# Second layer's queries and keys projected ahead of its loop and fetched per batch

## The chip, the cores and the metric

One core of a Trainium2 chip runs the whole program in one launch. The metric is device time in microseconds (us). Engines: PE (TensorE, with its weight loads PEld), DVE (VectorE), ACT (ScalarE), POOL (GpSimd), and SP, which here only issues DMAs. Each engine takes its instructions in order and waits on semaphores for the others.

## The reference, cut to what matters

Two transformer layers over x of 32 batches x 256 rows x 128 features, with a layer norm behind each of the four parts:

```python
# layer 0: x = LN(x + attention(x)); qkv with bias and a low-rank part, 16 heads of depth 8
# then     x = LN(x + experts(x)):
probs = softmax(x @ gate_w.T); top2_w, top2_idx = top_k(probs, 2)
counts = bincount(a_e, length=E); keep = counts <= cap      # cap = 1.25 * rows / E
contrib = y[a_e, p] * (a_w * valid)                         # 0 for an expert over its capacity
# layer 1: x = LN(x + attention(x)), causal, no bias, queries and keys rotated:
q = q * cos + _rotate_half(q) * sin
k = k * cos + _rotate_half(k) * sin
att = softmax(where(causal, q @ k.T * scale, min)); y = (att @ v) @ w_proj
# then     x = LN(x + ffn(x)), a spline feed-forward part
```

## The kernel before, in words

x lies in SBUF as 64 tiles of 128 rows (x_all, x_mid); a batch is two tiles. Five stages follow each other: `prepare`, `attention` for layer 0 (attn0), `moe`, `attention` for layer 1 (attn1), `spline_ffn`.

`attention` is a software pipeline over batches: step b works on batch b (transpose x, project queries and keys, split each into three bf16 parts and send them through DRAM, whence they come back stacked in q_st and k_st, L215), on batch b-2 (scores by rows, L558, and their maximum on DVE, L376), on b-3 (scores by columns, L580, exponential on ACT, L317, sums of values, L597) and on b-4 (normalise, output projection L537, residual L429, layer norm). Steps 0 to 4 fill it, a hardware loop of three steps a round follows, and some written-out steps drain it at the end. Within a step PE, ACT and DVE go through 16 turns n = 0 to 15 (one head or one half of two heads each); the table `AT` says at which turn each other piece comes. PE holds the row scores in three PSUM banks (`ROW_BANKS`): rows(u) waits until DVE's row_max(u-3) is done. cols(n) waits for the exponential n-2.

In attn1 before, for batch b of step b: SP copies x from x_mid into x_in (L195); PE transposes it at n = 0 (L481) into in_ps; ACT copies it to xT (L323); PE projects queries and keys at n = 1 (L502) into in_ps; ACT, at n = 2, writes q_half with the two halves of the partitions exchanged (L339, two copies of 64x512) and qk (L345, two of 128x256); POOL waits for these four (`qk_kept`) and then multiplies q_half by sin (L261), qk by cos (L262), adds (L265), and splits (L271 to L283). PE's value projection (L524, n = 4) waits for the same four copies, since it writes in_ps. At the end of each step, behind that work, POOL makes the variance and rstd of batch b-4 (L289, L291, a power). DVE's order at n = 15 is: row_max(15), residual and statistics (L429, L433), split of the maxima (L387, L389), aggregate (L439), and the two L444, which wait for rstd and write x_mid; row_max(0) of the next step stands behind them. In attn0 the layer norm is made by POOL instead (L297, L301).

`moe`: SP copies x_all in groups of eight tiles (L748), PE transposes them (L785), projects the gates (L797) and transposes back (L807); DVE measures mean and variance (L727 to L735) and copies logits (L868). Then one chain on DVE over all 64 tiles finds the two best experts and their counts (L876 to L903), PE adds the counts, and DVE makes a flag (L907 to L909): is any expert within its capacity? ACT (L845) and DVE (L915) write x_mid, the second layer norm. A second block does the experts' work if the flag is set; here it isn't.

## Time and profile before

| | us |
|---|---|
| median of three runs (lowest, highest) | 1361.35 (1359.0, 1361.97) |
| the profiled execution, its own time | 1361.33 |
| its span, first to last instruction | 1359.6 |
| layer 0's attention ends, moe begins | 540.5, 541.8 |
| layer 1's attention begins | 591.3 |

| engine | busy us | share of the span |
|---|---|---|
| PE | 1081.3 | 80% |
| DVE | 1029.6 | 76% |
| ACT | 835.7 | 61% |
| POOL | 582.8 | 43% |

A share of the whole span mixes stages: read it by stretch. In a timeline row stand the start and the length in us, the engine, the line, the operation, out<-in, partitions x elements, how many instructions were merged (x2), and in brackets how long the engine had been idle and who ended that. The duration of a row is that of the merged run.

### The profile page before, as it was taken

The page shows a single profiled execution, that of the slowest core. Times are in us where ns is not written, and L with a number is a line of the kernel's source. Part 1 is how long each engine was busy: PE and PEld are TensorE (multiplying, and loading weights), DVE is VectorE, ACT ScalarE, POOL GpSimd, SP SyncE. Part 2 cuts the span into 40 slices and gives each one's busy share as a digit, 9 for nine tenths or more (in the row PEclk, how much of TensorE's full clock was granted, in tenths as well). Part 3 has the DMA queues.
Part 4 walks back from the last instruction along what each step waited for, and adds up shares of the span by engine and source line. Part 5 has one row for each costly group of instructions (what it writes and reads, how often), then busy time and mean ns, then how long its engine had stood idle before and what let it go on. Part 6 is the DMA issues. An engine that isn't in the chain of part 4 may idle for free. (4 is left out here: it accounts for less than half of the span.)

```text
span 1359.6 us, 36441 instructions
## 1 busy us (share of the span) xinstructions
PE 1081.3 (80%) x11411; PEld 799.5 (59%) x11411; DVE 1029.6 (76%) x2823; ACT 835.7 (61%) x1904; POOL 582.8 (43%) x696
## 2 busy tenths in 40 slices
PE   2699999999999996516999999999999996501330
PEld 1366666666666663314888888888888873201220
DVE  3578888888888883824787788877888763698885
ACT  1267777777777774552666776767767664401675
POOL 3234434444444432434555555555555506000776
PEclk9799999999999998756999999999999998855555
DMA  2655555565556540305444554444554412100011
GB/s 57 151 122 136 131 139 128 133 140 131 136 135 137 135 100 10 115 29 134 120 119 121 119 123 120 116 121 119 124 119 120 115 35 82 43 0 0 24 47 54
DMA packets 122613, 137.33 MB, mean 101 GB/s; under 512 B 12562, under 2 KB 110258, under 8 KB 113330
## 3 DMA queue, kind: packets, MB, share of 16 engines
q1 hardware_dynamic: 121506, 136.50, 40.6%
q8 instruction: 34, 0.56, 0.2%
q14 instruction: 33, 0.27, 0.1%
q10 hardware_dynamic: 1040, 0.00, 0.0%
HBM read 85.03 MB, written 37.75 MB: 90 GB/s over the span
## 5 line engine op out<-in xcount | busy, mean ns | idle before, releaser
L376 DVE TENSOR_REDUCE attn_negmax<-attn_row_ps 128x2 f32<-128x512 f32 (+1 forms) x1024 | 597.8, 618 | 151.4 <-PE attn_row_ps L558 136.4
L317 ACT ACTIVATE attn_probs<-attn_col_ps 128x512 f32<-128x512 f32 (+1 forms) x1024 | 534.9, 546 | 111.8 <-PE attn_col_ps L580 106.5
L558 PE MATMUL attn_row_ps<-k_st,q_st 72*128 72x256 bf16 (+1 forms) x2048 | 370.3, 263 | 14.9 <-DMA k_st<-attn_scratch 13.9
L580 PE MATMUL attn_col_ps<-q_st,k_st 74*128 74x256 bf16 (+1 forms) x2048 | 369.8, 262 | 2.6 <-ACT attn_probs L317 2.0
L597 PE MATMUL attn_out_ps<-attn_probs,v_sb 128*32 128x256 f32 (+1 forms) x4096 | 230.4, 358 | 0.7 <-ACT attn_probs L317 0.7
L580 PEld LDWEIGHTS attn_col_ps<-q_st,k_st 74*128 74x128 bf16 x2048 | 184.3, 99 | 73.9 <-ACT attn_probs L317 23.2
L558 PEld LDWEIGHTS attn_row_ps<-k_st,q_st 72*128 72x128 bf16 x2048 | 201.9, 99 | 41.3 <-issue 15.3
L597 PEld LDWEIGHTS attn_out_ps<-attn_probs,v_sb 128*32 128x32 f32 x4096 | 123.3, 110 | 71.2 <-issue 21.3
L554 PE MATMUL attn_row_ps<-mask_qk,ident_h 128*128 128x256 bf16 x512 | 141.5, 276 | 19.1 <-DMA k_st<-attn_scratch 18.0
L576 PE MATMUL attn_col_ps<-mask_kq,ident_h 128*128 128x256 bf16 x512 | 141.3, 276 | 1.2 <-ACT attn_probs L317 1.0
L289 POOL TENSOR_SCALAR attn_var<-attn_mv 128x2 f32<-128x2 f32 x64 | 14.3, 223 | 265.8 <-DVE attn_mv L439 265.8
L276 POOL TENSOR_TENSOR attn_rest<-attn_qk,attn_parts 128x512 f32<-128x512 f32 x64 | 73.9, 1154 | 122.8 <-DVE attn_mparts L389 118.0
L261 POOL TENSOR_TENSOR attn_q_half<-attn_q_half,sin 128x512 f32<-128x512 f32 x32 | 40.7, 1273 | 136.4 <-ACT attn_qk L345 136.4
L502 PE MATMUL attn_in_ps<-attn_xT,wqk 128*128 128x256 f32 x256 | 79.6, 437 | 2.4 <-ACT attn_xT L323 2.4
L1552 POOL TENSOR_TENSOR ffn_rstd<-ffn_var,minus_half 128x8 f32<-128x8 f32 x19 | 31.8, 1674 | 106.6 <-DVE ffn_var L1574 105.2
L283 POOL TENSOR_TENSOR attn_parts<-attn_rest,attn_parts 128x512 bf16<-128x512 f32 x64 | 73.9, 1154 | 5.4
L271 POOL TENSOR_SCALAR attn_parts<-attn_qk 128x512 bf16<-128x512 f32 x64 | 39.5, 617 | 63.1 <-ACT attn_qk L342 49.2
L554 PEld LDWEIGHTS attn_row_ps<-mask_qk,ident_h 128*128 128x128 bf16 x512 | 49.6, 97 | 28.7 <-issue 18.7
L1482 PE MATMUL ffn_o_ps<-ident_h,ffn_onehot 128*128 128x128 bf16 x64 | 10.0, 312 | 70.2 <-PEq L1233 70.2
L1493 PE MATMUL ffn_r_ps<-table_hm,ffn_ohT 128*128 128x193 bf16 x64 | 21.0, 361 | 55.8 <-ACT ffn_ohT L1505 55.8
L356 ACT COPY attn_onT_sb<-attn_fin_ps 128x256 f32<-128x256 f32 x64 | 23.7, 370 | 60.2 <-PE attn_fin_ps L531 60.2
L576 PEld LDWEIGHTS attn_col_ps<-mask_kq,ident_h 128*128 128x128 bf16 x512 | 49.6, 97 | 16.1 <-issue 6.5
(230 smaller groups left out, 1689.0 us busy)
## 6 DMA issues: line engine op xcount, KB each, us to landing
q_st<-attn_scratch SPq DMA_DIRECT2D x192, 192.0 KB
k_st<-attn_scratch SPq DMA_DIRECT2D x192, 192.0 KB
attn_scratch<-attn_parts SPq DMA_DIRECT2D x64, 384.0 KB, 2.8
attn_scratch<-attn_parts SPq DMA_DIRECT2D x64, 128.0 KB, 2.9
x_in<-in_L_attn_x_dram SPq DMA_DIRECT2D x32, 128.0 KB, 2.6
x_all<-in_L_attn_x_dram SPq DMA_DIRECT2D x32, 128.0 KB, 7.0
moe_xs<-x_all SPq DMA_DIRECT2D x8, 512.0 KB, 2.9
x_in<-x_mid SPq DMA_DIRECT2D x32, 128.0 KB, 2.4
```

Source lines behind the costliest of these rows:

```text
L261: nc.gpsimd.tensor_tensor(q_half[:, :, :], q_half[:, :, :], sin, ALU.mult).then_inc(sin_done, 1)
L271: nc.gpsimd.tensor_scalar(parts[:, :, 0, :], qk[:, :, :], 1.0, 0.0, ALU.mult, ALU.add)\
L276: nc.gpsimd.tensor_tensor(rest[:, :, :], qk[:, :, :], parts[:, :, 0, :], ALU.subtract)\
L283: nc.gpsimd.tensor_tensor(parts[:, :, 2, :], rest[:, :, :], parts[:, :, 1, :], ALU.subtract)\
L317: nc.scalar.activation(probs_of(st, 3, u)[:, j, 0:W], col_ps[:, n % 2, 0:W], ACT.Exp, scale=scale).then_inc(probs_kept, 1)
L376: nc.vector.tensor_reduce(negmax[:, t, 2 * p:2 * p + 2], row_ps[:, row_bank(st, u), 0:2 * keys].rearrange("p (a k) -> p a k", a=2), AX_X, ...
L502: last = nc.tensor.matmul(in_ps[:, s * N:(s + 1) * N], wqk[:, s, :], xT[:, st.slot(0), :], start=True, stop=True)
L554: nc.tensor.matmul(seen[:, :, keys - P:keys], ident_h[:, :], mask_qk[:, :, :], start=True, stop=False, skip_group_check=True)
L558: last = nc.tensor.matmul(bank[:, a * keys:(a + 1) * keys], q_st[0:KROWS, sl, h, t * P:(t + 1) * P], k_st[0:KROWS, sl, h, 0:keys], start=n ...
L576: nc.tensor.matmul(seen[:, :, 0:P], ident_h[:, :], mask_kq[:, :, :], start=True, stop=False, skip_group_check=True)
L580: last = nc.tensor.matmul(bank[:, t * N:(t + 1) * N - first], k_st[0:rows, sl, h, t * P:(t + 1) * P], q_st[0:rows, sl, h, first:N], start= ...
L597: last = nc.tensor.matmul(out_ps[32 * j:32 * j + 32, g * N + first:(g + 1) * N], v_sb[:, st.slot(lag), t, 32 * h:32 * h + 32], probs_of(st ...
```

## The change

It has four parts. (1) In attn0 POOL, behind each batch's layer norm, works out the reciprocal deviation that the second layer norm will have (from rstd and the variance, `r_mid`) and writes x_mid = x_all * r_mid at once. (2) `moe` has no statistics, no copies through SP and no layer norm of its own: PE transposes x_mid straight into xT_all, which takes x_all's place in SBUF, and the logits are multiplied by 1/r_mid. The groups are written out; ACT copies the logits; the routing chain runs in two halves of 32 tiles. If the flag is set, x_all is restored and the transposes are made again. (3) attn1 has no transposes and no projection of queries and keys in its loop. Ahead of it PE projects batches 0 to 19 from xT_all into col_ps, and batches 20 to 31 in step 2, one a turn, n = 0 to 11. ACT copies 0 to 2 to qk and q_half; the others go into the buffers of probs and from there, four batches to a DMA from ACT's queue, to DRAM. (4) In the loop SP copies xT (128 KB) at a step's start and fetches qk of the next batch (256 KB) behind the six stack loads; ACT writes q_half from qk at n = 14; qk and q_half have three slots, so POOL waits only for copies made one step ahead (`half_kept`). DVE's copy of the values moves from n = 4 to 5.

```diff
@@ AT, attn1
-      "attn1": dict(act_xT=0, act_mT1=1, act_qk=(2, 2), act_oT=(4, 5), act_onT=13, act_mT0=9,
-                    dve_o=9, dve_split0=7, dve_split1=15, dve_v=4, dve_y=15, dve_var=15, dve_ln=15,
-                    pe_xT=0, pe_mT1=2, pe_qk=1, pe_oT=7, pe_v=4, pe_onT=11, pe_mT0=9, pe_y=15,
+      "attn1": dict(act_mT1=1, act_oT=(4, 5), act_half=14, act_onT=13, act_mT0=9,
+                    dve_o=9, dve_split0=7, dve_split1=15, dve_v=5, dve_y=15, dve_var=15, dve_ln=15,
+                    pe_mT1=2, pe_oT=7, pe_v=4, pe_onT=11, pe_mT0=9, pe_y=15,
...
+FRONT_GROUP = 4
+FRONT_EARLY = 20
@@ attention, sync
+            def load_xT(st):
+
+                if st.has(3):
+                    sp.wait_ge(v_ready, st.seq(3, c=1))
+                sp.dma_start(xT[:, st.slot(0), :], xT_all[:, bass.ds(st.seq(0), 1), :].rearrange("p b n -> p (b n)"))\
+                    .then_inc(x_loaded[st.slot(0)], 16)
+
+            def load_qk(st):
+
+                sp.wait_ge(rest_kept, st.seq(2, c=1))
...
+                sl = st.slot(-1)
+                of = qk_dram[bass.ds(st.seq(-1), 1)].rearrange("b p n -> (b p) n")
+                sp.dma_start(qk[:, sl, :, :].rearrange("p s n -> p (s n)"), of).then_inc(qk_loaded[sl], 16)
...
+                if fronted and st.has(-1) and (st.loop or st.off >= AHEAD):
+                    load_qk(st)
@@ attention, gpsimd
-                    pool.wait_ge(qk_kept, st.seq(0, QKOPS, QKOPS))
+                    if not fronted:
+                        pool.wait_ge(qk_kept, st.seq(0, QKOPS, QKOPS))
+                    elif st.loop or st.off >= SLOTS:
+                        pool.wait_ge(half_kept, st.seq(SLOTS, 2, 2))
+                    else:
+                        pool.wait_ge(front_kept, kept_by(st.off))
...
+                        nc.gpsimd.tensor_tensor(square[:, :], rstd[:, :], rstd[:, :], ALU.mult).then_inc(again, 1)
+                        pool.wait_ge(again, st.seq(4, 5, 1))
+                        nc.gpsimd.tensor_tensor(square[:, :], square[:, :], mv[:, :, 1], ALU.mult).then_inc(again, 1)
+                        pool.wait_ge(again, st.seq(4, 5, 2))
+                        apart(pool, mem)
+                        nc.gpsimd.tensor_scalar(square[:, :], square[:, :], EPS, 0.0, ALU.add, ALU.add)\
+                            .then_inc(again, 1)
+                        pool.wait_ge(again, st.seq(4, 5, 3))
+                        r_mid = mem["r_mid"][:, bass.ds(st.seq(4, TB), TB)]
+                        nc.gpsimd.tensor_tensor(r_mid, square[:, :], mem["minus_half"][:, 0:TB], ALU.pow)\
+                            .then_inc(again, 1)
...
+                        nc.gpsimd.tensor_tensor(mem["x_mid"][:, bass.ds(st.seq(4, TB), TB), :],
+                                                x_all[:, bass.ds(st.seq(4, TB), TB), :],
+                                                r_mid.unsqueeze(2).broadcast_to([P, TB, C]), ALU.mult)\
+                            .then_inc(again, 1)
@@ attention, scalar
+            def front(b):
+
+                act.wait_ge(front_ready, b + 1)
+                of = col_ps[:, b % 2, :]
+                if b < SLOTS:
+
+                    nc.scalar.copy(qk[:, b, :, :].rearrange("p s n -> p (s n)"), of).then_inc(front_kept, 1)
+                    for to, of_row in ((0, P // 2), (P // 2, 0)):
+                        nc.scalar.copy(q_half[to:to + P // 2, b, :, :].rearrange("p s n -> p (s n)"),
+                                       of[of_row:of_row + P // 2, :]).then_inc(front_kept, 1)
+                    return
...
+                nc.scalar.copy(staged(b), of).then_inc(front_kept, 1)
...
+                    act.dma_start(qk_dram[first:to].rearrange("b p n -> p b n"), probs[:, n, 0:to - first, :])\
+                        .then_inc(front_stored[group], 16)
...
+                            if fronted and not st.loop and st.off == 3:
+                                for stored in front_stored:
+                                    act.wait_ge(stored, 16)
...
+                    if fronted and n == at["act_half"] and st.has(-1) and (st.loop or st.off >= SLOTS - 1):
+                        sl = st.slot(-1)
+                        act.wait_ge(qk_loaded[sl], st.turn(-1, 16 * QK_LOADS, -16 * QK_LOADS))
+                        for to, of_row in ((0, P // 2), (P // 2, 0)):
+                            nc.scalar.copy(q_half[to:to + P // 2, sl, :, :].rearrange("p s n -> p (s n)"),
+                                           qk[of_row:of_row + P // 2, sl, :, :].rearrange("p s n -> p (s n)"))\
+                                .then_inc(half_kept, 1)
@@ attention, tensor
+            def front(b):
+
+                if b >= 2:
+                    pe.wait_ge(front_kept, kept_by(b - 2))
+                for s in range(2):
+                    last = nc.tensor.matmul(col_ps[:, b % 2, s * N:(s + 1) * N], wqk[:, s, :], xT_all[:, b, :],
+                                            start=True, stop=True)
+                last.then_inc(front_ready, 1)
...
                 for n in range(H):
+                    if fronted and not st.loop and st.off == 2 and FRONT_EARLY + n < B:
+                        front(FRONT_EARLY + n)
@@ moe
...
+                            last = nc.tensor.transpose(t_ps[:, j, t // 4, t % 4 * P:(t % 4 + 1) * P],
+                                                       x_mid[:, st.off * GT + t, :], ident[:, :])
...
+                            nc.scalar.copy(xT_flat[:, at:at + 512], t_ps[:, j, b, :]).then_inc(xT_kept, 1)
...
+                nc.vector.reciprocal(r_inv[:, :], r_mid[:, :]).then_inc(mean_kept, 1)
+                dve.wait_ge(mean_kept, 1)
+                dve.wait_ge(consts, E + 2)
+                route(0)
+                route(1)
```

## Rows read from the trace of the kernel before

**Rows 1.** Busy time by stretch, second layer's loop; columns us busy (count), clock, DMA, GB/s.
```profile
748.00:850.00 102.00, 100.50 (x1223) 83.96 (x1215) 82.40 (x210) 71.22 (x173) 56.09 (x61) 1.00 0.50 121
```

**Rows 2.** Timeline of POOL, second layer: variance of steps 4, 31 and 32.
```profile
668.63 0.22 POOL L289 TENSOR_SCALAR attn_var<-attn_mv 128x2 f32<-128x2 f32 x1 [3.29 <-DVE attn_mv L439]
...
1085.39 0.22 POOL L289 TENSOR_SCALAR attn_var<-attn_mv 128x2 f32<-128x2 f32 x1 [3.28 <-DVE attn_mv L439]
...
1099.68 0.22 POOL L289 TENSOR_SCALAR attn_var<-attn_mv 128x2 f32<-128x2 f32 x1 [13.27 <-DVE attn_mv L439]
```

**Rows 3.** Timeline of all engines, one step boundary in the second layer's loop.
```profile
821.54 0.41 DVE L429 TENSOR_TENSOR attn_y_sb<-attn_fin_ps,x_mid 128x256 f32<-128x256 f32 x1
...
822.60 1.13 PE L502 MATMUL attn_in_ps<-attn_xT,wqk 128*128 128x256 f32 x4
...
823.55 0.71 POOL L291 TENSOR_TENSOR attn_rstd<-attn_var,minus_half 128x2 f32<-128x2 f32 x1
...
824.30 0.60 DVE L444 TENSOR_SCALAR x_mid<-attn_y_sb,attn_mv,attn_rstd 128x128 f32 x2 [1.25 <-POOL attn_rstd L291]
...
824.82 1.34 DVE L376 TENSOR_REDUCE attn_negmax<-attn_row_ps 128x2 f32<-128x256 f32 x3
...
825.25 1.18 ACT L339 COPY attn_q_half<-attn_in_ps 64x512 f32<-64x512 f32 x2
...
825.97 0.27 PE L554 MATMUL attn_row_ps<-mask_qk,ident_h 128*128 128x256 bf16 x1
...
827.15 0.52 PEld L524 LDWEIGHTS attn_in_ps<-wv,attn_xT 128*128 128x128 f32 x4 [0.36 <-ACT attn_qk L345]
...
827.25 1.28 POOL L261 TENSOR_TENSOR attn_q_half<-attn_q_half,sin 128x512 f32<-128x512 f32 x1 [2.99 <-ACT attn_qk L345]
...
827.98 0.27 PE L554 MATMUL attn_row_ps<-mask_qk,ident_h 128*128 128x256 bf16 x1
...
828.48 1.29 POOL L262 TENSOR_TENSOR attn_qk<-attn_qk,cos 128x512 f32<-128x512 f32 x1
```

**Rows 4.** Timeline of all engines, from layer one's end to layer two's start.
```profile
539.91 0.61 POOL L301 TENSOR_TENSOR x_all<-attn_y_sb,attn_rstd 128x256 f32<-128x256 f32 x1
...
545.04 1.97 PE L785 MATMUL moe_t_ps<-ident,moe_xs 128*128 128x128 f32 x8 [8.54 <-DMA moe_xs<-x_all]
...
568.51 0.23 DVE L868 COPY moe_logits<-moe_l_ps 128x64 f32<-128x64 f32 x1 [0.65 <-PE moe_l_ps L807]
568.77 0.69 DVE L876 TENSOR_REDUCE moe_top<-moe_logits 128x64 f32<-128x512 f32 x1
...
583.87 0.15 DVE L909 CAST moe_flag<-moe_any_kept 128x1 int32<-128x1 f32 x1
...
587.04 2.27 DVE L915 TENSOR_SCALAR x_mid<-x_all,moe_mean,moe_rstd  x8 [0.28 <-issue]
591.28 1.50 SPq L195 DMA_DIRECT2D x_in<-x_mid  x2
```

**Rows 5.** Group of the page (busy, mean ns, idle before): POOL's remainder, both layers.
```profile
L276 POOL TENSOR_TENSOR attn_rest<-attn_qk,attn_parts 128x512 f32<-128x512 f32 x64 | 73.9, 1154 | 122.8 <-DVE attn_mparts L389 118.0
```

**Rows 6.** Timeline of PE: first score rows of layer two.
```profile
620.18 0.37 PE L554 MATMUL attn_row_ps<-mask_qk,ident_h 128*128 128x256 bf16 x1 [18.00 <-DMA k_st<-attn_scratch]
```

**Rows 7.** Busy time by stretch (columns as in rows 1): one microsecond within the loop.
```profile
834.00:835.00 1.00, 1.00 (x13) 0.89 (x12) 0.97 (x2) 0.65 (x3) 0.92 (x2) 1.00 0.03 8
```

**Rows 8.** Timeline of DVE and POOL: two DVE ops beside POOL's L265 and L1542.
```profile
829.92 1.27 POOL L265 TENSOR_TENSOR attn_qk<-attn_qk,attn_q_half 128x512 f32<-128x512 f32 x1
...
830.35 0.87 DVE L387 CAST attn_mparts<-attn_negmax 128x16 bf16<-128x16 f32 x1
...
1340.55 1.65 POOL L1552 TENSOR_TENSOR ffn_rstd<-ffn_var,minus_half 128x8 f32<-128x8 f32 x1
1342.17 1.26 POOL L1542 TENSOR_TENSOR ffn_z<-ffn_z,gamma 128x512 f32<-128x512 f32 x1
1342.23 1.22 DVE L1579 SCALAR_TENSOR_TENSOR ffn_shift<-ffn_mv,ffn_rstd 128x8 f32<-128x8 f32 x1 [1.76 <-POOL ffn_rstd L1552]
```

More of the change, by code:

```diff
@@ L331, in step @@
                     for s in range(2):
-                        if n == at["act_qk"][s] and st.has(0):
+                        if not fronted and n == at["act_qk"][s] and st.has(0):
                             if s == 0:
@@ L362, in step @@
                             .then_inc(mT_kept, 1)
+            if fronted:
+                for b in range(FRONT_EARLY):
+                    front(b)
             pipeline(act, step)
@@ L518, in project_v @@
             def project_v(st):
-                if st.has(0):
+                if fronted:
+                    pe.wait_ge(x_loaded[st.slot(2)], st.turn(2))
+                if st.has(0) and not fronted:
                     pe.wait_ge(qk_kept, st.seq(0, QKOPS, QKOPS))
-                else:
+                elif st.has(3):
                     pe.wait_ge(mT_kept, st.seq(3, 2, 1))
@@ L609, in step @@
                         score_rows(st, n)
-                    if n == at["pe_xT"] and st.has(0):
+                    if not fronted and n == at["pe_xT"] and st.has(0):
                         transpose_x(st)
@@ L616, in step @@
                             sum_values(st, lag, u)
-                    if n == at["pe_qk"] and st.has(0):
+                    if not fronted and n == at["pe_qk"] and st.has(0):
                         project_qk(st)
@@ L631, in step @@
                         project_o(st)
+            if fronted:
+                for b in range(FRONT_EARLY):
+                    front(b)
             pipeline(pe, step)
@@ L640, with groups @@
 GROUPS = TILES // GT
-LN_SPLIT = 6
+HALF = TILES // 2
 MT = 4
-def groups(eng, step):
-    pipeline(eng, step, 2, 4, GROUPS, 0)
+def groups(step):
+    for n in range(GROUPS + 3):
+        step(Step(0, n, 2, GROUPS))
 def moe(nc, mem, w):
-    x_all, x_mid, ident = mem["x_all"], mem["x_mid"], mem["ident"]
+    x_all, x_mid, xT_all, r_mid, ident = (mem[k] for k in ("x_all", "x_mid", "xT_all", "r_mid", "ident"))
+    xT_flat = xT_all[:, :, :].rearrange("p b n -> p (b n)")
     with ExitStack() as ctx:
@@ L704, in moe @@
         l_ps = ctx.enter_context(nc.psum_tensor("moe_l_ps", [P, 2, 512], F32))
[L706 removed]
+        loaded, consts = sem("loaded"), sem("consts")
         xT_ready, xT_kept, gates_ready, gates_kept, logits_ready, logits_kept = (
@@ L738, in moe @@
         with nc.Block() as block:
-            @block.sync
-            def _(sp):
-                def step(st):
-                    if st.has(0):
-                        j = st.slot(0)
-                        wait(sp, xT_ready, st.seq(1))
-                        sp.dma_start(xs[:, j, :, :], x_all[:, bass.ds(st.seq(0, GT), GT), :])\
-                            .then_inc(xs_loaded[j], 16)
-                groups(sp, step)
             @block.gpsimd
```

285 lines of the change are left out of this document (151 added, 134 removed).

## The prediction

> **What bounds the kernel now.** I read the busy time by stretch first. In the second layer's loop TensorE (PE) is busy 100.5 of 102 us at clock 1.00, DVE 82.4, ACT 71.2, POOL 56.1 [rows 1]. So PE paces that loop, and DVE is the next one: 12.5 us of each step. Then the starts of POOL's variance, one a step, give the step: from step 4 to step 31 (1085.39 - 668.63)/27 = 15.44 us. Step 32, in which no new batch enters, so no x transposed, no queries and keys projected, no rotation on POOL, takes 1099.68 - 1085.39 = 14.29 us [rows 2]. This is the most that emptying the loop's front can give: 1.15 us a step, 27 x 1.15 = 31 us. Then the step boundary in order of time [rows 3]: who holds whom there decides the change. Last the stage between the layers [rows 4], where DVE's chain ends last and PE hardly works.
>
> The sum is made on the profiled span, 1359.6 us; that execution took 1361.33, so 1.7 lie outside it, and 1361.33 is the median of the three runs shown to 0.02 us. About 0.2% (2.7 us) is what a measurement of this kernel can tell from no change.
>
> **First layer.** POOL gets five ops more per batch behind L301: two products and a sum on 128x2, a power on 128x2 (0.71 us, as L291 [rows 3]) and a product on 128x256 (0.61, as L301 [rows 4]). With 0.22 to 0.3 for each of the small ones (L289 takes 0.22 [rows 2]) and 0.15 behind each own wait that is 2.6 us. POOL's next timed op, L276, has 122.8 us of idle time in front of it in 64 executions, nearly all for DVE's L389 [rows 5]: 1.9 us on average over both layers and more here, where the second layer's front has none to spare. I take the loop as unchanged (0); without that cover up to 27 x 0.7 = 19 us. The last batch has no cover: +2.6 us (bounds +2 to +3.5).
>
> **Experts stage.** Removed: the copies of x_all through SP (PE starts at 545.04, after a DMA wait, 4.5 us after L301's end at 540.52), DVE's statistics, and the last normalisation behind the flag: from 584.02 to 589.31 [rows 4], 5.3 us. PE now starts some 1.3 us after the block opens, so 544.4 with the 2.6 above. The eight groups took 568.74 - 545.04 = 23.7 us, paced by DVE's statistics; without them I take 20, so last logits at 564.4 (bound: 568). The routing chain ran from 568.77 to 584.02, 15.3 us at 512 elements an op (0.69 us, L876); an op on 256 takes 0.41 (L429 [rows 3]), so each half's 18 ops at 0.46 with the trip to ACT take 9.7 us. The first half starts near 558, ends 568; the second, not started before, ends 577.5; count, flag and the 1.97 us from L915's end to the next layer (591.28) bring layer two to 580.5: **-10.8 us**, the 2.6 included (bounds -6 to -13).
>
> **Second layer's fill.** Before, 28.9 us go from 591.28 to the first score rows at 620.18 [rows 4, 6], which wait for DMA behind POOL's first chain. After it PE projects at once (L502's four take 1.13 us warm [rows 3], about twice that cold, as L785's 1.97 for eight shows against the rest), and POOL starts some 4 us earlier; but 29 batches go to DRAM at 256 KB each and share the engines with the first stacks. I take the first rows 1 us earlier. ACT's eight DMA issues stand between copies that wait for PE anyway. New waits: ACT's first exponential of step 3 waits for all stores, the last of them issued some 4 us earlier, and holds every exponential behind it (0 to 3 us); SP's load of xT waits for a value projection of the step before, and holds nothing. Step 2 then holds twelve projections more, 12 x 1.0 = 12 us on PE against about 7 of transposes, waits and cold projections that leave steps 2 to 4: **+2 us** after all (bounds -4 to +10).
>
> **The loop, step 5 to 31.** Out of PE's queue: L502 (1.13 us), two transposes (0.2) and the wait of 0.36 at L524 for ACT [rows 3]; step 32 caps this at 1.15. ACT loses three copies at n = 0 and 2, and writes both exchanged halves (1.18 us, L339 [rows 3]) at n = 14; behind them in ACT's queue stands the exponential n = 15, which cols(1) of the next step waits for: 0.5 us back. SP issues 256 KB more a step behind the six stack loads. The DMA engines are idle again at 834 (share 0.03 [rows 7]), and ACT wants the data at about 836: 256 KB at a mean share of 0.50 for 121 GB/s [rows 1] are 1.1 us, so they arrive in time. Bounds 0 to 1 us a step; I take 0.
>
> **A new neighbour for DVE.** Before, POOL's first rotation op L261 started 3 us after the rstd (827.25 against 824.26), since it waited for ACT's copies. Now its input is ready a step ahead, so L261 follows L291 directly, at about 824.24. At that moment DVE's two L444 start (824.30), which also wait for L291 [rows 3]. What such a meeting costs is shown twice [rows 8]: L387, 16 elements, started at 830.35 under L265 and took 0.87, ending at 831.22 when L265 ended (831.19); and behind the power L1552 POOL's next op L1542 started 0.03 us before its end, DVE's L1579 waiting for the same power started 0.06 later and took 1.22, until L1542 ended. This is our pattern exactly. So the first L444 ends at 825.6 instead of 824.65. POOL's L262 has no wait in front of it and takes the place next; the second L444 then ends behind it, at about 826.9 instead of 824.90. (The Trainium skill, "SBUF — State Buffer", section "Who interferes with whom", says that the port pair shared by VectorE and GpSimd is an exclusive lock held for the whole instruction, and that a VectorE tensor_scalar in a 2-port mode takes it. By that rule L444 waits; the trace agrees for L387, which ended with L265. It speaks against this change.)
>
> Who waits for that: row_max(0) stands behind L444 on DVE and ends at 827.25 instead of 825.24; PE has three banks of rows, so rows(3) waits for it: 827.3 against 825.97, +1.3. Behind it on PE rows(4) waits for row_max(1), 827.9, and rows(5) comes at 829.05 instead of 827.98 [rows 3]. From there PE is at its own pace. Saved work is used up before: it only makes PE reach rows(3) sooner. So +1.07 us a step, 27 x 1.07 = **+29 us**. (Gained is 0.7 at L387, now at an idle POOL, but DVE is not late there.)
>
> Sum: 1359.6 - 10.8 + 2 + 29 = 1379.8, with 1.7 outside 1381.5. Forecast **1381 us**.
>
> **Rivals.**
> - One block only: the second L444 slips in between L261 and L262. Then LN ends near 825.85, row_max(0) at 826.2, rows(5) at 828.05: +0.05 a step, +1. 1359.6 - 10.8 + 2 + 1 + 1.7 = 1354. This ends on the other side, faster. It decides at whether DVE's second op is ready within about 0.1 us after its first; L444's two starts lie (0.60 - 0.34) = 0.26 apart, which speaks against it.
> - No block (L444 gets through first, or POOL starts later): rows(3) at 825.5, rows(5) at 827.25, -0.65 a step, -18: 1334. L1542 speaks against it, and that SP's fetch would have to be over 2 us late.
> - Both L444 lose to two ops of POOL, or PE's longer gap at rows(3) costs more: LN ends at 828.3, +2.4 a step, +65: 1418.
> - The fetch is late: 256 KB stand between the stack loads and the small rows of maxima in the same queue; if qk arrives 1 us after ACT's turn at n = 14, all exponentials wait, +1 a step on top: about 1400.
> - That the loop isn't relieved at all is excluded by step 32 [rows 2].
>
> **How the numbers follow.** Two blocks 0.49 (1381), one 0.20 (1354), none 0.09 (1334), more than two 0.11 (1418), late fetch 0.11 (1400). The range reaches from the one-block case with the bounds of the experts stage, 1346, to 1408, between the late fetch and the three-block case; outside lie the no-block case and most of the 1418 case, about 0.19. The likeliest case alone: 1370 to 1392. Faster than 1358.6: none, and four fifths of one block, and a little of the first: 0.28; within 0.2%: 0.05; slower 0.67.
>
> **What would show it.** L444 with means of about 1 us instead of 0.34, L261 starting within 0.1 us of L291's end; L554's idle time released by DVE; step spacing near 16.5 us (15.5 with one block, 14.8 with none); L387 at 0.17 in both places; the layer starting near 580; PE's busy share in the loop falling from 98.5% to about 87%. The forecast is wrong if L444 keeps 0.34, if the fill grows by more than 10 us through the DRAM stores, or if ACT waits for the fetch.

## The result and the profile after

The changed kernel takes 1383.38 us (median of four runs, 1377.89 to 1385.31), the kernel before 1360.88 us (1359.0 to 1361.97) beside it: a ratio of 1.016, with an interval of [1.0127, 1.0193]. It is slower by 1.6%; 1381 was forecast. The profiled execution took 1385.31 us with a span of 1383.6, 24.0 more than the span before. It is the slowest of the four, 2 us above the median; the account below is of this one execution.

The page of the changed kernel, some of its lines (slices of 34.6 us; groups with count, busy time, mean and the idle time in front of them):

```profile
span 1383.6 us, 36076 instructions
...
PE 1081.5 (78%) x11349; PEld 797.7 (58%) x11349; DVE 1033.6 (75%) x2676; ACT 816.3 (59%) x1801; POOL 627.8 (45%) x845
...
PEclk9799999999999998798999999999999998855555
...
L656 PE MATMUL attn_row_ps<-mask_qk,ident_h 128*128 128x256 bf16 x512 | 143.4, 280 | 47.4 <-DVE attn_negmax L476 41.1
...
L678 PE MATMUL attn_col_ps<-mask_kq,ident_h 128*128 128x256 bf16 x512 | 143.3, 280 | 24.0 <-ACT attn_probs L414 23.6
...
L544 DVE TENSOR_SCALAR x_mid<-attn_y_sb,attn_mv,attn_rstd 128x128 f32 (+1 forms) x64 | 71.2, 1153 | 39.8 <-POOL attn_rstd L341 39.8
...
attn_qk<-attn_qk_scratch SPq DMA_DIRECT2D x29, 256.0 KB, 7.2
attn_qk_scratch<-attn_probs ACTq DMA_DIRECT2D x7, 1024.0 KB, 7.6
```

In the changed file L312, L313 and L316 are POOL's rotation (L261, L262 and L265 before), L339 and L341 its variance and rstd (L289, L291), L544 is DVE's normalisation (L444), L476 its row maximum (L376), L656 and L678 open PE's score rows and columns (L554, L576), L414 is ACT's exponential and L451 its copies of exchanged halves. PE does as much as before, 1081.5 us, but waits 41 us for DVE's row maxima and 24 us for ACT's exponentials. L544 takes 1153 ns in the mean.

Where the 24.0 us lie, by the starts of POOL's variance L339 and of SP's first issue in the second layer (the timeline of the changed kernel, POOL and SP):

```profile
536.48 0.22 POOL L339 TENSOR_SCALAR attn_var<-attn_mv 128x2 f32<-128x2 f32 x1 [2.56 <-DVE attn_mv L539]
...
577.90 0.60 SPq L225 DMA_DIRECT2D attn_xT<-x_all  x1
...
663.52 0.22 POOL L339 TENSOR_SCALAR attn_var<-attn_mv 128x2 f32<-128x2 f32 x1 [4.27 <-DVE attn_mv L539]
...
825.91 0.22 POOL L339 TENSOR_SCALAR attn_var<-attn_mv 128x2 f32<-128x2 f32 x1 [4.44 <-DVE attn_mv L539]
...
843.74 0.22 POOL L339 TENSOR_SCALAR attn_var<-attn_mv 128x2 f32<-128x2 f32 x1 [4.61 <-DVE attn_mv L539]
...
1109.89 0.22 POOL L339 TENSOR_SCALAR attn_var<-attn_mv 128x2 f32<-128x2 f32 x1 [4.28 <-DVE attn_mv L539]
```

Before, the first layer's last variance stood at 538.07 (timeline of POOL in the kernel before):

```profile
538.07 0.22 POOL L289 TENSOR_SCALAR attn_var<-attn_mv 128x2 f32<-128x2 f32 x1 [5.60 <-DVE attn_mv L439]
```

The second layer began at 591.28 [rows 4], and the variances of steps 4 and 31 stood at 668.63 and 1085.39 [rows 2]. So:

| stretch | before, us | after, us | difference | forecast |
|---|---|---|---|---|
| first layer, to its last variance | 538.07 | 536.48 | -1.6 | 0 |
| from there to the second layer | 53.21 | 41.42 | -11.8 | -10.8 |
| second layer's fill, to the variance of step 4 | 77.35 | 85.62 | +8.3 | +2 |
| 27 steps | 416.76 | 446.37 | +29.6 | +29 |
| the rest | 274.2 | 273.7 | -0.5 | 0 |

A step boundary of the changed kernel (timeline of all engines, 744 to 750.3), to be laid beside [rows 3]:

```profile
744.02 0.28 PE L678 MATMUL attn_col_ps<-mask_kq,ident_h 128*128 128x256 bf16 x1 [0.64 <-ACT attn_probs L414]
...
744.70 0.22 POOL L339 TENSOR_SCALAR attn_var<-attn_mv 128x2 f32<-128x2 f32 x1 [4.36 <-DVE attn_mv L539]
...
745.00 0.71 POOL L341 TENSOR_TENSOR attn_rstd<-attn_var,minus_half 128x2 f32<-128x2 f32 x1
...
745.68 1.29 POOL L312 TENSOR_TENSOR attn_q_half<-attn_q_half,sin 128x512 f32<-128x512 f32 x1
745.74 2.54 DVE L544 TENSOR_SCALAR x_mid<-attn_y_sb,attn_mv,attn_rstd 128x128 f32 x2 [1.25 <-POOL attn_rstd L341]
...
746.94 1.26 POOL L313 TENSOR_TENSOR attn_qk<-attn_qk,cos 128x512 f32<-128x512 f32 x1
...
748.20 2.27 DVE L476 TENSOR_REDUCE attn_negmax<-attn_row_ps 128x2 f32<-128x256 f32 x5
...
748.67 0.28 PE L656 MATMUL attn_row_ps<-mask_qk,ident_h 128*128 128x256 bf16 x1 [1.48 <-DVE attn_negmax L476]
...
750.29 0.27 PE L656 MATMUL attn_row_ps<-mask_qk,ident_h 128*128 128x256 bf16 x1
```

The reader is to see the chain that was forecast: L312 starts 0.03 us before the end of the power, DVE's pair 0.06 us later, and takes 2.54 us instead of 0.60, ending 0.08 after L313's end; the row maxima behind it start at once (the rows of the first three had been ready); PE stands still for 1.48 us at rows(3), and ACT's copies at n = 14 cost PE another 0.64 us at cols(1). The pair takes 2.5 us in all 27 steps from 4 to 30 and 0.60 in the five behind, which no new batch follows. 22 of the 27 steps take 16.2 to 16.3 us (16.23 in the mean), and five take 17.8 to 17.9. What is special about those five stands in the granted clock (windows of PE; columns: length, busy time, granted clock, DMA share, GB/s), here from 828 to 836:

```profile
828.00:830.00 2.00, 0.45 (x5) 1.00 0.47 139
830.00:831.00 1.00, 1.00 (x12) 1.00 0.90 188
831.00:832.00 1.00, 1.00 (x9) 0.62 0.65 115
832.00:833.00 1.00, 1.00 (x7) 0.50 1.04 201
833.00:834.00 1.00, 1.00 (x8) 0.50 0.85 193
834.00:835.00 1.00, 1.00 (x8) 0.67 0.71 147
835.00:836.00 1.00, 1.00 (x13) 1.00 0.73 145
```

PE's gap of 1.55 us at rows(3) ended at 829.87. About 1.4 us later the clock fell to half, 1.2 GHz, for 3.4 us, though PE was busy again. In the boundary at 748 above, with a gap of 1.48 us, it stayed at 1.00, and so it did in other steps with 1.55.

### The profile page after: what moved, and what is told of

Its sections match the earlier page's. It is cut to its first block and busy times, and to the rows that moved or that the text cites. A ratio compares the mean times of both kernels' runs of the same rounds, so it can differ in the third digit from the quotient of the medians.

```text
span 1383.6 us, 36076 instructions
## 1 busy us (share of the span) xinstructions
PE 1081.5 (78%) x11349; PEld 797.7 (58%) x11349; DVE 1033.6 (75%) x2676; ACT 816.3 (59%) x1801; POOL 627.8 (45%) x845
## 5 line engine op out<-in xcount | busy, mean ns | idle before, releaser
L476 DVE TENSOR_REDUCE attn_negmax<-attn_row_ps 128x2 f32<-128x512 f32 (+1 forms) x1024 | 596.2, 618 | 178.1 <-PE attn_row_ps L660 169.1
L414 ACT ACTIVATE attn_probs<-attn_col_ps 128x512 f32<-128x512 f32 (+1 forms) x1024 | 535.1, 544 | 188.7 <-PE attn_col_ps L682 179.4
L660 PE MATMUL attn_row_ps<-k_st,q_st 72*128 72x256 bf16 (+1 forms) x2048 | 372.6, 264 | 14.6 <-DMA k_st<-attn_scratch 13.8
L656 PE MATMUL attn_row_ps<-mask_qk,ident_h 128*128 128x256 bf16 x512 | 143.4, 280 | 47.4 <-DVE attn_negmax L476 41.1
L699 PEld LDWEIGHTS attn_out_ps<-attn_probs,v_sb 128*32 128x32 f32 x4096 | 123.9, 110 | 71.4 <-issue 21.3
L678 PE MATMUL attn_col_ps<-mask_kq,ident_h 128*128 128x256 bf16 x512 | 143.3, 280 | 24.0 <-ACT attn_probs L414 23.6
L339 POOL TENSOR_SCALAR attn_var<-attn_mv 128x2 f32<-128x2 f32 x64 | 14.3, 223 | 290.6 <-DVE attn_mv L539 290.6
L544 DVE TENSOR_SCALAR x_mid<-attn_y_sb,attn_mv,attn_rstd 128x128 f32 (+1 forms) x64 | 71.2, 1153 | 39.8 <-POOL attn_rstd L341 39.8
L656 PEld LDWEIGHTS attn_row_ps<-mask_qk,ident_h 128*128 128x128 bf16 x512 | 50.3, 98 | 63.6 <-DVE attn_negmax L476 47.9
L678 PEld LDWEIGHTS attn_col_ps<-mask_kq,ident_h 128*128 128x128 bf16 x512 | 50.0, 98 | 43.7 <-ACT attn_probs L414 30.4
L312 POOL TENSOR_TENSOR attn_q_half<-attn_q_half,sin 128x512 f32<-128x512 f32 x32 | 41.0, 1280 | 45.0 <-ACT attn_q_half L385 38.6
```

The lines of the kernel that those rows point to most:

```text
L312: nc.gpsimd.tensor_tensor(q_half_, q_half_, sin, ALU.mult).then_inc(sin_done, 1)
L414: nc.scalar.activation(probs_of(st, 3, u)[:, j, 0:W], col_ps[:, n % 2, 0:W], ACT.Exp, scale=scale).then_inc(probs_kept, 1)
L476: nc.vector.tensor_reduce(negmax[:, t, 2 * p:2 * p + 2], row_ps[:, row_bank(st, u), 0:2 * keys].rearrange("p (a k) -> p a k", a=2), AX_X, ...
L544: nc.vector.tensor_scalar(x_all[:, bass.ds(st.seq(4, TB, t), 1), :].rearrange("p t c -> p (t c)"), y_sb[:, t, :], mv[:, t, 0:1], rstd[:, t ...
L656: nc.tensor.matmul(seen[:, :, keys - P:keys], ident_h[:, :], mask_qk[:, :, :], start=True, stop=False, skip_group_check=True)
L660: last = nc.tensor.matmul(bank[:, a * keys:(a + 1) * keys], q_st[0:KROWS, sl, h, t * P:(t + 1) * P], k_st[0:KROWS, sl, h, 0:keys], start=n ...
```

## The experiments

The theory at this point: the loop is slower because DVE's two ops meet two ops of POOL; nothing else of the change matters in the loop. The rivals: the fetch or ACT's copies; POOL's timing in general; the emptied front. The edits below are against the changed kernel unless said otherwise, and each ratio is to the kernel before, timed on the same chip; between chips that kernel's own median differs by up to 4 us (1357.71 to 1361.38), so ratios are compared across experiments rather than times.

**Without the meeting.** POOL's first rotation op waits for DVE's pair of the step before.

```
+                    if rope and st.has(5):
+                        pool.wait_ge(ln_kept, st.seq(5, TB, TB))
                     if rope:
```

> The changed kernel, in which POOL starts the rotation of the next batch (L312) only after DVE's two normalising ops (L544) of the step before. Theory A (the two ops of DVE meet two ops of POOL): L544 falls back from 1.15 to 0.34 us in the mean (a pair in 0.60 instead of 2.54), PE's gap of 1.5 us at rows(3) goes, the step falls from 16.53 to about 14.8 us (15.44 before, less the relief of PE seen in step 32, with ACT's copies given back), and the time from 1383 to 1383 - 27 x 1.73 = about 1337. The five long steps (17.85 us, granted clock 0.50 for some 3.5 us behind PE's gap) go too. Theory B (the gap of PE comes from the fetched queries and keys or from ACT's copies at n = 14): L544 gets fast, the step stays at 16.2 or more, the time at 1375 to 1385. Theory C (POOL, starting 0.6 us later, becomes late for the stacks): PE waits for k_st or DVE for POOL in the loop, step 15.5, about 1355.

Measured: 1333.95 us, ratio 0.9795 [0.9756, 0.9834]. Its boundary (timeline; L341 and L343 are variance and rstd, L546 the pair, L314 the first rotation op):

```profile
826.28 0.71 POOL L343 TENSOR_TENSOR attn_rstd<-attn_var,minus_half 128x2 f32<-128x2 f32 x1
...
827.02 0.60 DVE L546 TENSOR_SCALAR x_mid<-attn_y_sb,attn_mv,attn_rstd 128x128 f32 x2 [1.25 <-POOL attn_rstd L343]
...
827.54 2.33 DVE L478 TENSOR_REDUCE attn_negmax<-attn_row_ps 128x2 f32<-128x256 f32 x5
...
827.77 1.27 POOL L314 TENSOR_TENSOR attn_q_half<-attn_q_half,sin 128x512 f32<-128x512 f32 x1 [0.79 <-DVE x_mid L546]
```

The pair is back at 0.60, PE no longer waits at rows(3), the step is (1060.30 - 664.27)/27 = 14.67 us, none is long. POOL's op, which had followed the rstd at once, now waits 0.79 us for the pair, and nobody is late for it. One wait is worth 49 us and turns the loss into a gain of 2%. Theories B and C fall.

With the shorter step another wait appears, for the fetched queries and keys, in front of ACT's copies of exchanged halves (L453 here; timeline of ACT):

```profile
720.85 1.26 ACT L453 COPY attn_q_half<-attn_qk 64x512 f32<-64x512 f32 x2 [0.30 <-DMA attn_qk<-attn_qk_scratch]
```

In the changed kernel's loop each fetch lands 1.3 us or more before ACT's copy. Here 12 of 26 copies wait for it, 0.12 to 0.47 us, 2.8 us in all; the 27 steps together are 2.6 us longer than 27 times their most frequent length, 14.57 us.

**The meeting alone.** In the kernel before, POOL gets one or two products of 128x512 on tiles that nobody reads, right behind the rstd; the only difference between the two is `range(1)` or `range(2)`, with POOL's own wait counted to match.

```
+                    if rope:
...
+                        wait(pool, near_done, st.seq(4, 2))
+                        for k in range(2):
+                            nc.gpsimd.tensor_tensor(near[k][:, :, :], cos, sin, ALU.mult).then_inc(near_done, 1)
```

> The kernel before, with one more op on POOL in the second layer's loop (a product of 128x512 on a tile that nobody reads) right behind the power L291, so that it starts together with DVE's first L444. Theory A (one block): one L444 of each pair takes about 1.3 us, the other 0.34, the normalisation ends 1.0 us later, the row maximum behind it is in time for PE but for 0 to 0.1 us: step 15.44 to 15.55, time 1361 to 1365. Theory B (the pair loses twice even to one op, or each late us of DVE is a us of PE): step 16.4, time 1388.

> The kernel before, with two such ops back to back behind L291, nothing else changed. Theory A (each L444 is held by one op of POOL): a pair takes 2.5 us instead of 0.60, PE waits 1.3 to 1.8 us at rows(3) for row_max(0), step 15.44 + 1.07 = 16.5, time 1361 + 29 = 1390; where PE's gap lowers the granted clock in some steps, 8 us more. Theory B (the price in the changed kernel comes from its emptied front, not from the meeting): L444 slow, but the step at 15.5 to 15.8, time 1362 to 1371.

Measured: 1365.81 us with one, ratio 1.0029 [1.0011, 1.0046]; 1391.31 us with two, ratio 1.0227 [1.0187, 1.0268]. The pair in the two kernels (timeline; L451 is the pair, L561 opens PE's rows, L299 is the added work), first one op, then two:

```profile
842.42 1.29 POOL L299 TENSOR_TENSOR attn_near<-cos,sin 128x512 f32<-128x512 f32 x1
...
842.49 1.56 DVE L451 TENSOR_SCALAR x_mid<-attn_y_sb,attn_mv,attn_rstd 128x128 f32 x2 [1.25 <-POOL attn_rstd L293]
```

```profile
843.00 2.50 POOL L299 TENSOR_TENSOR attn_near<-cos,sin 128x512 f32<-128x512 f32 x2
...
843.06 2.52 DVE L451 TENSOR_SCALAR x_mid<-attn_y_sb,attn_mv,attn_rstd 128x128 f32 x2 [1.25 <-POOL attn_rstd L293]
...
845.97 0.28 PE L561 MATMUL attn_row_ps<-mask_qk,ident_h 128*128 128x256 bf16 x1 [1.06 <-DVE attn_negmax L383]
```

Each op of POOL holds one op of DVE until about 0.08 us after its own end: with one the first of the pair is held and the second slips through (1.56), with two both are held (2.52). With one the step stays at 15.44, the slack takes it all; the time is 4 us longer, and 3.6 of them lie behind these 27 steps, where the added op runs too: the two steps without a new batch take 15.22 each instead of 14.29 and 14.57. With two the step is (1101.58 - 663.44)/27 = 16.23. That is the changed kernel's 16.2 to 16.3, reached with the old front. PE's gap is 1.0 to 1.1 us here, since the projection still fills a part of it, and none of the 27 steps is long. The 1390 that was expected is met in part by luck: the 27 steps give 21 us and not 29, and the four steps behind them, which have the added ops too, give another 11 (56.8 us against 45.5).

**One block in the changed kernel.** L312 starts as it did, only L313 waits for DVE's pair.

```
                         nc.gpsimd.tensor_tensor(q_half_, q_half_, sin, ALU.mult).then_inc(sin_done, 1)
+                        if st.has(5):
+                            pool.wait_ge(ln_kept, st.seq(5, TB, TB))
                         nc.gpsimd.tensor_tensor(qk_, qk_, cos, ALU.mult).then_inc(cos_done, 1)
```

> The changed kernel, in which only POOL's second op (L313) waits for DVE's two normalising ops; the first, L312, still starts with them. Theory A (blocks count one by one, and PE has slack for one): a pair of L544 takes 1.55 us, as the pair did in the kernel before with one op added there, row_max(0) ends 1 us later than in the kernel without a meeting, where PE reached rows(3) without a wait; PE's gap is 0.3 us or less, the step 14.65 to 14.95, no fall of the granted clock, time 1335 to 1342. Theory B (in the emptied front even one block reaches PE in full, since PE comes to rows(3) 1.1 us sooner than in the kernel before): step 15.6, time 1360.

Measured: 1350.75 us, ratio 0.9918 [0.9899, 0.9936]; the pair takes 1.56 us, PE's gap is 0.50 us, the step (1075.60 - 663.50)/27 = 15.26. Neither theory had it: one block costs 0.6 us here, none in the old kernel. The kernels so far give a rule for this loop. A step runs in a ring: rows(3), PE's work up to the output projection, residual and statistics, POOL's variance and rstd, DVE's pair, row_max(0), rows(3). With the pair's time taken off, the ring's length is 16.23 - 2.54, 16.23 - 2.52 and 15.26 - 1.56: 13.69, 13.71, 13.70 us. Against it stands PE's own pace, 15.44 with the old front and 14.67 with the new (0.64 for ACT's copies and 0.1 for the fetch included). The longer of the two is the step. So the first block is free in the old kernel (13.70 + 1.56 = 15.26 is below 15.44) and costs 0.6 in the new one. The ring also explains step 32 [rows 2], without a new batch: 13.70 + 0.60 = 14.30 beside a measured 14.29, and PE waits 0.34 us at the rows there. The 14.29 from which the prediction took the most that an empty front can give is thus the ring's length with the pair at 0.60, and no step of this loop in any of the kernels is shorter than 14.27.

**DVE late without a meeting.** POOL's wait as in the first experiment; DVE does seven more ops of the pair's kind in front of the pair.

```
+                for k in range(7):
+                    nc.vector.tensor_scalar(late[:, k, :], y_sb[:, k % TB, :], mv[:, 0, 0:1], rstd[:, 0:1],
+                                            ALU.subtract, ALU.mult).then_inc(late_done, 1)
```

> The changed kernel with POOL's wait, so without a meeting; DVE does seven more ops like L544 (128x128, on a tile that nobody reads) between the rstd and its two ops, 7 x 0.26 = 1.8 us. From four kernels I have step = 13.69 + (time from the first normalising op to the end of the last), where that is above PE's own pace (15.44 with the old front, 14.6 with the new). Theory A (the meeting costs only the lateness of DVE, by this sum): 13.69 + 2.44 = 16.1 us a step, PE's gap about 1.4 us, 1334 + 27 x 1.5 = 1374, and where the granted clock falls behind such a gap in some steps, up to 10 us more. Theory B (the meeting itself costs PE or POOL something beyond DVE's lateness): step 15.7 or less, 1363.

Measured: 1390.43 us, ratio 1.0225 [1.0194, 1.0257]. From the first extra op to the pair's end it takes 2.39 us (783.99 to 786.38), PE's gap is 1.33 to 1.53 us, and the undisturbed steps take 16.07 to 16.27: the ring gives 13.70 + 2.39 = 16.1 (the first extra op also starts 0.13 us behind the power, the pair 0.04). Long steps are back, 19.41 us once (clock 0.50 for 6.8 us) and 17.81 once (3.4 us) among the 27, with no meeting anywhere. The total is above the expectation's 1374 to 1384 since it counted 27 steps: the steps behind them (1108.09 to 1164.53, 56.4 us against 45.5 in the first experiment) do the extra ops too. So DVE's lateness is all that the meeting costs the loop, and the long steps go with PE's gap and need no meeting.

**ACT's two copies apart**, with POOL's wait: one behind n = 14, one behind n = 15.

```
-                    if fronted and n == at["act_half"] and st.has(-1) ...
+                    if fronted and n in at["act_half"] and st.has(-1) ...
...
-                        for to, of_row in ((0, P // 2), (P // 2, 0)):
+                        for to, of_row in (((0, P // 2), (P // 2, 0))[n - 14],):
```

> The changed kernel with POOL's wait for the normalisation, and ACT's two copies of exchanged halves apart: one behind the exponential n = 14, one behind n = 15. Theory A (PE's 0.64 us at cols(1) for ACT is the pair of copies in one piece): that wait goes, the step falls from 14.63 to the 14.28 of the steps without a new batch, 27 x 0.35 = 9 us: 1325. Theory B (what ACT gives, another wait takes, the row maxima or the values' copies): step 14.55 or more, 1331 to 1334.

Measured: 1330.45 us, ratio 0.9765 [0.974, 0.979], step (1056.31 - 664.11)/27 = 14.53 against 14.67. The direction is A's, the size 0.14 of the 0.35 us; most steps are at 14.28 to 14.48, every third or so at 14.6 to 14.7 and one at 15.86. What takes the rest is in large part another wait, as theory B said, but none of those that it named: it is the fetch. 15 of 26 first copies wait for it, 4.9 us in all, and the longest of these waits stands in the step of 15.86:

```profile
677.58 0.62 ACT L453 COPY attn_q_half<-attn_qk 64x512 f32<-64x512 f32 x1 [1.63 <-DMA attn_qk<-attn_qk_scratch]
```

The interval overlaps that of the kernel without the split, so the trace carries this reading, not the times.

**How much of the front runs ahead of step 2**: FRONT_EARLY = 26 or 16 in place of 20, with POOL's wait.

> The changed kernel with POOL's wait for the normalisation; of the 32 projections ahead of the loop 26 instead of 20 run before step 2, so 6 instead of 12 inside it. Theory A (PE stands idle for 6 us before the first score rows, and there the six are free): first score rows near 608 as before, step 2 shorter by 6 x 1.2 = 7 us, the last store to DRAM is issued earlier, and ACT's wait of 4 us for the stores at the start of step 3 shrinks: 7 to 10 us less, 1324 to 1327. Theory B (the stores are 1 MB each and share the DMA engines with the first stacks): the first score rows come 3 to 5 us later, gain 2 to 4, 1330 to 1332.

> The same with 16 projections before step 2 and 16 inside it. Theory A: step 2 grows by 4 x 1.2 us, ACT's wait for the stores stays 4 us or grows: 1339 to 1342. Theory B (fewer stores in front of the first stacks): first score rows 2 to 4 us earlier, the total within 2 us of 1334.

Measured: 1332.35 us (0.9775 [0.9747, 0.9803]) and 1336.67 us (0.9817 [0.9792, 0.9842]) against 1333.95. From the layer's start to the variance of step 4 it takes 84.7 us with 26, 85.9 with 20, 88.6 with 16. With 26 PE no longer idles before its first rows, which come no later (25.75 us after POOL's first op, 25.64 before), but 1.1 us are left of the 7 expected: ACT then stands 9.17 us in front of its copy for the fetched queries and keys, and PE 7.44 for the small rows of maxima. The projections in step 2 were not what made the fill long; behind them ACT and PE stand for DMA traffic. Neither theory for 26 named ACT's wait for the fetch. With 16 the result lies between its two theories. The intervals of the three kernels overlap, so this too is read from the traces, one execution of each.

**Each store to DRAM twice**, the second to a spare region, with POOL's wait.

```
...
+                    act.dma_start(spare_dram[first:to].rearrange("b p n -> p b n"), probs[:, n, 0:to - first, :])\
+                        .then_inc(front_stored[group], 16)
```

> The changed kernel with POOL's wait; each of the eight stores of queries and keys to DRAM is issued twice, the second to a region that nobody reads, and whoever waits for a store waits for both: 7.25 MB more in the fill. Theory A (the stores' bytes on the DMA engines are what makes the fill long; they run at 300 to 370 GB/s there): 7.25 MB at 340 GB/s are 21 us, of which 4 to 10 hide beside the projections: the fill, from the start of the layer to the first variance (85.9 us), grows by 11 to 20 us, time 1345 to 1354. Theory B (the fill is long for the twelve projections in step 2 and PE's low clock; the stores are hidden): it grows by 3 us or less, 1334 to 1337.

Measured: 1348.58 us, ratio 0.9924 [0.99, 0.9949]. The fill takes 103.3 us (578.19 to 681.46) instead of 85.9, the first score rows come at 612.25 instead of 608.06, and ACT stands 8.35 us for the stores. The DMA engines in the changed kernel and in this one (windows; columns: length, clock, DMA share, GB/s):

```profile
590.00:600.00 10.00, 1.00 1.01 318
600.00:607.00 7.00, 0.93 0.99 312
```

```profile
600.00:607.00 7.00, 1.00 1.02 293
607.00:615.00 8.00, 0.69 1.03 337
615.00:624.00 9.00, 0.90 1.06 388
624.00:632.00 8.00, 0.69 1.03 322
632.00:640.00 8.00, 0.88 1.03 383
```

The engines are full (share 0.99 to 1.06) at 312 and 318 GB/s in the changed kernel's fill and at 293 to 388 here; 7.25 MB more cost 17.4 us. (The Trainium skill, "DMA: Bandwidth & Descriptors", "Specifications", gives a limit of about 358 GB/s of HBM for a core. The rows lie from 293 to 388, so around it and in part above; the measurement decides.)

**Waiting only for the stores that matter**, on top of POOL's wait and the copies apart: ACT's exponentials of step 3 overwrite the tiles that the stores read, four tiles, two stores each.

```
-                                for stored in front_stored:
+                                for stored in front_stored[u::PROBS]:
```

> As the kernel with POOL's wait and the two copies apart (1330.5), and ACT's exponentials of step 3 wait only for the stores that read the four tiles they overwrite: the first four for two of the eight stores, not for all. Theory A (the 4.2 us that ACT stands in front of the first exponential, for the last store, are the fill's): the exponential starts when cols(0) is there, PE's gap of 3.0 us goes and with it the fall of the granted clock behind it: 3 to 6 us less, 1325 to 1327. Theory B (the bytes of the stores are the cost, and the next wait is the fetch of step 4 or the last groups' stores): 0 to 1.5 us less, 1329 to 1330.5.

Measured: 1324.65 us, ratio 0.9735 [0.9705, 0.9765]. The fill takes 81.0 us (574.89 to 655.92) instead of 85.8, and the granted clock from 620 to 664 is 0.96 instead of 0.88. In the changed kernel and in this one ACT's first exponential of step 3 reads:

```profile
630.21 0.87 ACT L414 ACTIVATE attn_probs<-attn_col_ps 128x384 f32<-128x384 f32 x2 [4.01 <-DMA attn_qk_scratch<-attn_probs]
```

```profile
623.55 0.99 ACT L416 ACTIVATE attn_probs<-attn_col_ps 128x384 f32<-128x384 f32 x2 [0.86 <-PE attn_col_ps L684]
```

In the kernel without this edit the clock stood at 0.50 for 6.8 us from 630.6 on, where PE waited 3.0 us for ACT; here it has no such stretch. So the 4.8 us are this wait and the clock that fell with it, as far as one execution of each can say. A part comes back elsewhere: ACT now stands 2.66 us for the fetch in step 3, instead of 1.47.

**The first two parts alone**: first layer and experts stage of the changed kernel, the second layer's attention as before.

> The first layer and the experts stage of the changed kernel, with the second layer's attention as it was before. Theory A: the whole gain of the stage stands alone: the second layer starts at 577.9 instead of 591.28, its fill takes the 28.9 us to the first score rows as before, its steps 15.44 us: 1359.6 - 13.4 + 1.7 = 1348. My forecast had 10.8 for this term, which would be 1350.5. Theory B (half of the stage's gain hangs on the projections ahead, since the old front has a chain of its own behind the start): 1353 or more.

Measured: 1345.66 us, ratio 0.9881 [0.9841, 0.9921]. The stage takes 41.71 us, the fill 75.2 (579.38 to 654.62), the step 15.44. The stage's gain of 11.5 us stands alone; in the profiled execution the fill is 2.1 us shorter besides and the first layer ends 0.4 us sooner.

**POOL's wait, the copies apart and 26 projections ahead, together.**

> POOL's wait, the two copies of exchanged halves apart, and 26 projections before step 2, together. If the three add up as they did one by one (27 x 0.14 = 4 us for the copies, 1.1 us for the fill): 1334 - 5 = 1329; if the fetch, which ACT's first copy waits for in the fill, comes later than ACT's turn: 1331.

Measured: 1325.84 us, ratio 0.9754 [0.9733, 0.9775], step 14.52. As ratios they add up within the intervals (0.9795 less 0.0030 and 0.0020); the time in us is below the 1329 since the kernel before is 3 to 4 us faster on this chip than on those of the parts. The fill, though, takes 81.2 us where 84.7 was seen with 26 projections alone: a single execution's fill is not known to better than a few us. Beside the kernel with waits by store this is the same within the intervals, and both beat the kernel before by 2.5 to 2.7%.

## Why the prediction was right, point by point

- **The neighbour for DVE: right in mechanism and count, the price mis-sized.** L312 starts with the rstd's end, both ops of the pair are held, row_max(0) and rows(3) follow. rows(3) came 3.97 us after the variance (forecast 4.06) and rows(5) 5.59 (forecast 5.81), so a step costs 16.23 - 15.44 = 0.79 us, not 1.07 (0.09 us of the difference lie before rows(3), 0.13 between rows(3) and rows(5), and 0.06 are not placed); 27 x 0.79 = 21.3 us of the 29. The point of decision that was named ("whether DVE's second op is ready within about 0.1 us after its first") was not what decided: wherever POOL had a second op ready, it started 0.05 us before DVE's second op, in every step, and held it; with one op of POOL the second op of DVE got through.
- **A term that was missing: the clock.** Five of 27 steps were 1.6 us longer, 8.1 us in all, with a granted clock of 0.50 for 3.4 us behind the gap. The rival "PE's longer gap costs more" had a price for a normalisation still later, 2.4 us a step, and none for the clock. That 21.3 + 8.1 comes to 29.4 beside a forecast of 29 is luck: two errors of 8 us cancelled. How many long steps the other three executions had is not on record; they took 1377.89 to 1384.84 us.
- **"Saved work is used up before": right.** The old front and the new one have the same step with two blocks (16.23). Read from the ring, the projection and the transposes lie between the output projection and rows(3), in the stretch in which PE waits anyway. Once the meeting is gone the relief shows: 14.67 instead of 15.44.
- **The rivals.** No block was put at 1334; the kernel without the meeting took 1333.95, but with a step of 14.67 (14.79 in the forecast) and a fill 6 us longer than forecast, so its hit is in part chance too. One block was put at 1354 with 0.05 us a step above 15.44; measured are 1350.75 and 15.26, below. The late fetch does not happen in the changed kernel's loop; in the fill it does once (ACT waits 1.27 us for it in step 3). But the reason given for "they arrive in time" was wrong: 1.1 us was taken for the 256 KB, and from issue to landing they take 6.9 to 7.8 us in the loop, behind the six stack loads in the same queue. The step of 16.2 us leaves room for that; with the step of 14.67 the fetch is late in every second step or so, and this rival becomes true in small.
- **ACT's copies at n = 14:** 0.64 us at PE instead of 0.5. In the changed kernel this costs nothing, since PE has a gap behind it; without the meeting it is worth 0.14 us a step when the copies are apart, with the fetch late as it is.
- **L387:** 172 ns in the mean (326 before, over both layers), as forecast, and worth nothing to DVE.
- **First layer: right.** Its step is 14.72 us before and after, the five small ops have their cover. The tail from x_all's end to x_mid's end is 541.56 - 538.94 = 2.62 us against a forecast of 2.6. The 1.6 us by which the layer ends sooner can't be put down to the change: over the profiled kernels its first timed variance lies at 88.4 to 92.6 us, with the old code and the new, and 0.9 of the 1.6 lie before it; from there to its last it takes 445.5 us with the old code and 444.6 to 445.9 with the new.
- **Experts stage: right, a little too small.** 11.8 us instead of 10.8. The groups were ready sooner (the last logits at 560.8, forecast 564.4); the halves' routing took 9.4 and 9.2 us (forecast 9.7 each), and the second half began when the first was through, as forecast.
- **Fill: the wrong step.** +8.3 instead of +2. The first score rows came 0.7 us later after the layer's start than before, not 1 us earlier, though POOL began 3.7 us sooner: the stacks share full DMA engines with the stores. Twelve projections took 13.7 us in step 2, and the first columns of step 3 come 18.7 us after the first rows of step 2 instead of 12.7. ACT's wait for the stores was 4.01 us where 0 to 3 was allowed. The step of the working that failed is the twelve projections with the waits behind them, taken as 12 us against 7 saved, and the traffic of the stores, which was named but put at nothing beyond ACT's 0 to 3 us. The runs show 13.7 us for the projections, 4.01 for ACT, and 17.4 us for 7.25 MB of stores more. The fill itself varies: in the kernels with the old attention it takes 72.8 to 80.6 us, with the clock at 0.50 for longer or shorter, so a part of the difference of 6 us between forecast and measurement can be this. The whole span is 3.8 us above the forecast's 1379.8: 6.3 here and 0.6 in the loop, less 3.1 in the other stretches.
- **PE's busy share in the loop** is 84.6 of 97.4 us, 87%, as forecast.

## What to carry to other kernels

When work is moved out of a loop, what it did as a spacer goes too: list the ops that can now start at the same moment on VectorE and GpSimd, and let GpSimd wait until the one on the critical ring is through; here one wait was worth 49 us. Compute the step as the longer of each engine's own pace and of the ring of waits through the step's end, for then it can be read off which lateness is free (the first us in the old kernel) and which is paid in full. While the ring is the longer, a relief of the pacing engine counts only outside the stretch in which that engine waits for the ring. And take a transfer's time from issue to landing in its own queue, not from its bytes: 7.2 us here, not 1.1.

## What the runs showed of the hardware that was not expected

- **The granted clock can fall behind a gap of 1.5 us, and does so in some of equal steps.** With PE's gap at 1.45 to 1.55 us once in a step of 16.2, the clock fell to 0.50 for 3.4 us in 5 of 27 steps, each 1.6 us longer; in the kernel with DVE late (1.33 to 1.53 us) two steps were lengthened. With 1.1 us or 0.6 us in every step none of 27 was, nor behind the single gaps of 1.43 and 1.50 us in the two kernels with the copies apart (one of them with 26 projections ahead). With 2.1 to 2.2 us (the two steps without a new batch, in the kernel with two added ops and in the one with DVE late) all four were hit, with the clock at 0.50 for 3.4 or 6.8 us. Which of equal steps is hit was not settled, and each kernel was seen in one execution.
- **A meeting is counted in ops, not in time.** An op of 0.34 us on DVE took 1.30 us beside an op of 1.27 us on POOL, and two short ones back to back were held by two of POOL's, each ending 0.08 us behind POOL's; POOL's ops kept their 1.26 to 1.29 us. (The Trainium skill, "SBUF — State Buffer", "Who interferes with whom", says that issue order decides who blocks. The rows agree by their starts: POOL's first op starts 0.06 us before DVE's first, and its second 0.04 to 0.06 us before DVE's second, which starts 0.08 us before the end of DVE's first, in all 27 steps.)
- **The row maxima were not held.** Of the short ones (128x256) in the changed kernel's loop, 68 that lay wholly under an op of POOL took 0.41 to 0.43 us, and the 69 with none beside them the same.
- Stores of 1 MB each at 293 to 388 GB/s fill the 16 DMA engines. A fetch of 256 KB behind six stack loads of 192 KB takes 6.9 to 7.8 us from issue to landing in the loop, at a mean DMA share of 0.52; transfers of the same size in the last stage, without stacks in front, take 2.3 us in the median.
